# Gathering raw token rows with their mean and reciprocal deviation, instead of stored normalised rows

## The reference, cut to what matters

```python
def _layernorm(x, axis=-1, eps=1e-05):
    m = jnp.mean(x, axis=axis, keepdims=True)
    v = jnp.var(x, axis=axis, keepdims=True)
    return (x - m) / jnp.sqrt(v + eps)

def _L0_ffn_ref(x, router_W, router_b, W1, b1, W2, b2):
    logits = jnp.einsum('bsd,de->bse', x, router_W) + router_b
    probs = jax.nn.softmax(logits, axis=-1)
    mask = jax.nn.one_hot(jnp.argmax(probs, axis=-1), N_EXPERTS)      # 8 experts, top 1
    gates = mask * probs
    h = jax.nn.relu(jnp.einsum('bsd,edf->besf', x, W1) + b1[:, None, :])   # 128 -> 512
    y = jnp.einsum('besf,efd->besd', h, W2) + b2[:, None, :]               # 512 -> 128
    return jnp.einsum('bse,besd->bsd', gates, y)

x = x + 0.5 * _L0_ffn_ref(_layernorm(x, axis=-1), ...)
x = x + _L0_attn_ref(_layernorm(x, axis=-1), ...)
x = x + 0.5 * _L0_ffn_ref(_layernorm(x, axis=-1), ...)
```

## Time and profile before

| what | value |
|---|---|
| time, median of 3 | 206.65 us |
| span of the profiled execution | 213.1 us |
| busy in the span: PE, DVE, ACT, POOL | 188.7, 121.3, 111.6, 122.0 us |
| mean granted TensorE clock | 0.963 |
| DMA: moved, mean rate | 40.26 MB, 189 GB/s |
| chain that ended last, by engine | PE 63%, DVE 13%, issue 9%, POOL 6%, DMA 4%, ACT 2% |

### The profile page before, as it was taken

One profiled execution on the slowest core, in us unless ns is written; L12 is line 12 of the kernel. 1 busy time (PEld: TensorE's weight loads), 2 busy tenths in 40 slices (PEclk: granted clock), 3 DMA queues, 4 the chain that ended last, 5 costly groups with the idle time before them and its releaser, 6 DMA issues.

```text
span 213.1 us, 4561 instructions
## 1 busy us (share of the span) xinstructions
PE 188.7 (89%) x1410; PEld 159.3 (75%) x1410; DVE 121.3 (57%) x516; ACT 111.6 (52%) x328; POOL 122.0 (57%) x186
## 2 busy tenths in 40 slices
PE   4978599997999598898999999998996899999992
PEld 2953269986989597666876588698643899999991
DVE  4858312212212348789897946757531677777762
ACT  2666026644437455778869875131300666666670
POOL 6887456695555526834399704557673154455544
PEclk9976969999999969999999999999999999999998
DMA  5999679764778336169996000001018749676700
GB/s 191 242 381 342 208 249 342 256 197 134 243 174 286 81 85 178 41 259 415 418 410 250 0 2 3 27 28 43 27 63 285 257 165 306 206 264 223 248 27 0
DMA packets 26680, 40.26 MB, mean 189 GB/s; under 512 B 4229, under 2 KB 16296, under 8 KB 25632
## 3 DMA queue, kind: packets, MB, share of 16 engines
q1 hardware_dynamic: 21136, 33.01, 43.9%
q0 software_dynamic: 2496, 4.76, 8.3%
q10 hardware_dynamic: 3024, 2.20, 3.3%
HBM read 10.78 MB, written 14.46 MB: 118 GB/s over the span
## 4 chain that ended last, share of the span: by engine, by line
PE 63%; DVE 13%; issue 9%; POOL 6%; DMA 4%; ACT 2%; another core or an unknown queue 1%; POOLq 0%; DVEq 0%
PE bank L1102 20%; PE bank L1119 18%; PE bank L1238 6%; PE bank L1254 5%; DMA xn_scratch<-xn 3%; PE bank L1095 3%; PE bank L928 2%; DVE stat L1323 2%; POOL xn L581 1%; PE bank L1193 1%; PE bank L1179 1%; DMA Xg<-xn_scratch,srcu 1%; PE bank L1203 1%; DVE x L1558 1%; PE bank L1210 1%
## 5 line engine op out<-in xcount | busy, mean ns | idle before, releaser
L747 ACT ACTIVATE hT<-bank,ewc_own 128x128 f32<-128x128 f32 x184 | 51.6, 373 | 56.7 <-PE bank L1102 38.2
L1102 PE MATMUL bank<-xT,ewc_own 128*128 128x128 f32 x368 | 51.1, 284 | 6.5 <-DVE xT L1455 3.8
L1102 PEld LDWEIGHTS bank<-xT,ewc_own 128*128 128x128 f32 x368 | 46.3, 198 | 9.2 <-issue 9.2
L1119 PE MATMUL bank<-ew,hT 128*128 x368 | 49.4, 278 | 0.0
L1119 PEld LDWEIGHTS bank<-ew,hT 128*128 128x128 f32 x368 | 45.5, 195 | 0.2 <-issue 0.2
L681 POOL DMA_INDIRECT out_dram<-ysb,eqrq x23 | 22.6, 982 | 26.6 <-issue 17.6
L609 POOL DMA_INDIRECT Xg<-xn_scratch,srcu x23 | 22.0, 958 | 15.0 <-PE bank L1102 4.8
L1461 DVE TENSOR_TENSOR ysb<-bank,ewc_own 128x128 f32<-128x128 f32 x23 | 6.7, 289 | 34.1 <-PE bank L1119 26.5
L634 POOL DMA_INDIRECT xnT<-slot_scratch,posu x16 | 15.8, 987 | 13.5 <-DVE ysb L1461 4.3
L928 PE MATMUL bank<-ones_bf 128*128 128x512 bf16 x66 | 19.9, 428 | 3.1 <-POOL ident L499 2.7
L673 POOL DMA_INDIRECT row_scratch<-pay,posu x16 | 15.8, 987 | 10.8 <-DVE posu L1428 6.8
(11 more groups left out here) (239 smaller groups left out, 303.7 us busy)
## 6 DMA issues: line engine op xcount, KB each, us to landing
ewc_own<-ew SPq DMA_DIRECT2D x46, 322.0 KB
row_scratch<-xn SPq DMA_DIRECT2D x8, 1024.0 KB, 10.6
ew<-in_L_ffn_W_dram SPq DMA_DIRECT2D x1, 2048.0 KB, 11.1
slot_scratch<-ysb SPq DMA_DIRECT2D x23, 64.0 KB
ew<-in_L_ffn_W_dram SPq DMA_DIRECT2D x5, 256.0 KB, 9.4
eqrq<-row_scratch SPq DMA_DIRECT2D x18, 70.0 KB
x<-in_L_attn_x_dram SPq DMA_DIRECT2D x4, 256.0 KB, 3.6
xn_scratch<-xn ACTq DMA_DIRECT2D x4, 256.0 KB, 6.2
```

What stands on the lines that cost most here:

```text
L747: last = A(hT[:, t.slot, c * P:(c + 1) * P], up_bank(k, c)[:, c * P:(c + 1) * P], ACT.Relu, scale=0.5 if m else 1.0, bias=ewc[t.ahead][:, ...
L1102: last = mm(up_bank(k, c)[:, c * P:(c + 1) * P], ewc[t.ahead][:, c * P:(c + 1) * P], xT[:, t.slot, :], start=True, stop=True)
L1119: last = mm(bank[4 + t.parity][:, 0:D], hT[:, t.slot, c * P:(c + 1) * P], ew[:, bass.ds(e[k], 1), W2_AT + c * D:W2_AT + (c + 1) * D].squee ...
```

## The change

The first mixture layer now works as the second: a memory tensor `x_scratch` of 130 numbers a row takes the raw row, its mean and its reciprocal deviation, and VectorE normalises each gathered tile.

- SP copies x from the input to `x_scratch` in four transfers from memory to memory (rows of 512 bytes at a pitch of 520), after the first-layer weights and ahead of its five second-layer loads.
- ACT stores mean and reciprocal deviation of each group (`store_stats`, 512 pieces of 8 bytes each) between its copies; GpSimd writes the reciprocal deviation into `mv`, beside the mean.
- The normalised rows `xn`, their stores, ACT's `renormalise`, GpSimd's share of it and VectorE's `first_shift` go. Gathers go to `Xp`, a buffer that the second time uses too, and wait for the copies, the statistics and the list.
- `normal` runs in both expert stages, in the first one or two tiles ahead.
- ACT loads the second-layer weights of the last three experts only after the first tile's own weights have landed.
- In `ranks`, the four products that need later constants (two lines) move behind the first half's rank products, the wait of the first half is for fewer constants, and a product that only kept TensorE busy goes.
- GpSimd makes its masks and other constants before its three row-hit products, not after them. The constant rows that fill memory come from a buffer `filler`.

```diff
+XW = D + 2
-    xn_scr = nc.dram_tensor("xn_scratch", [TOK, D], f32, kind="Internal").ap()
+    x_scr = nc.dram_tensor("x_scratch", [TOK, XW], f32, kind="Internal").ap()
...
             sp.dma_start(ew[:, :, W1_AT:W1_AT + F], ew1_d.rearrange("e p f -> p e f")).then_inc(ew_in, 16)
+            for g in range(NG):
+                sp.dma_start(x_scr_v[:, g, :, 0:D], x_v[:, g, :, :]).then_inc(x_copied, 16)
             load_w2(sp, range(NE - W2_BY_ACT))
...
-            for t in range(POOL_ROWS * GT, (POOL_ROWS + 1) * GT):
-                last = g.tensor_scalar(xn[:, t, :], x[:, t, :], mv[:, t, 0:1], rstd[:, t, 0:1], ALU.subtract, ALU.mult)
-            last.then_inc(xn_by_pool, 1)
...
-                    g.indirect_dma_start(out=Xg[:, k % UNROLL, :], out_offset=None, in_=xn_scr,
+                    g.indirect_dma_start(out=Xp[:, k % UNROLL, 0:XW], out_offset=None, in_=x_scr,
...
-                for b in range(NG):
-                    pool.wait_ge(xn_stored[b], 16)
+                pool.wait_ge(x_copied, 16 * NG)
+                pool.wait_ge(stats_stored, 16 * NG)
                 pool.wait_ge(src_ready, 1)
...
+            def store_stats(g):
+
+                act.wait_ge(rstd_ready, g + 1)
+                act.dma_start(x_scr_v[:, g, :, MEAN_AT:XW], mv[:, g * GT:(g + 1) * GT, :]).then_inc(stats_stored, 16)
...
-            for g in range(NG):
+            take_xn(0, 0)
+            for g in range(1, NG):
                 take_xn(0, g)
-            renormalise(0)
-            renormalise(1)
-            store_xn(0)
-            store_xn(1)
-            renormalise(3)
-            store_xn(3)
-            store_xn(POOL_ROWS)
+                store_stats(g - 1)
+            store_stats(NG - 1)
             exponentials()
             row_hits()
+            act.wait_ge(ewc_in[0], 16)
             load_w2(act, range(NE - W2_BY_ACT, NE))
...
-                pe.wait_ge(const_ready, 10)
-                mm(bank[5][0:NV, 0:1], whole[:, :], ones_v[0:1, 0:1], start=True, stop=False, skip_group_check=True)
-                mm(bank[5][0:NV, 2:4], ident[0:NV, 0:NV], add_step[:, :], start=False, stop=False, skip_group_check=True)
+                pe.wait_ge(const_ready, 5)
...
                 for t in range(PICKED):
                     spread(t)
-                keep_warm(1)
+                pe.wait_ge(const_ready, 10)
+                mm(bank[5][0:NV, 0:1], whole[:, :], ones_v[0:1, 0:1], start=True, stop=False, skip_group_check=True)
+                mm(bank[5][0:NV, 2:4], ident[0:NV, 0:NV], add_step[:, :], start=False, stop=False, skip_group_check=True)
                 pe.wait_ge(oh_ready, picks(0))
...
-                    if m == 0:
-                        pe.wait_ge(g_in[t.ahead], 16 * (1 + t.round))
-                    else:
-                        pe.wait_ge(xg_ready, t.k + 1)
+                    pe.wait_ge(xg_ready, m * NT + t.k + 1)
...
-                    dve.wait_ge(xp_in[t.ahead], 16 * (1 + t.round))
+                    dve.wait_ge((xp_in if m else g_in)[t.ahead], 16 * (1 + t.round))
...
+                normal(0)
                 take_x(0)
-                if m == 1:
-                    normal(1)
+                normal(1)
                 take_x(1)
-                if m == 1:
-                    normal(2)
+                normal(2)
                 for k in range(NT):
...
                     for n in ups_before_down(m, k):
                         if n + 1 < NT:
                             take_x(n + 1)
+                        if m == 0 and n + 2 < NT:
+                            normal(n + 2)
```

53 lines of the change are left out of this document (14 added, 39 removed).

## The result

The changed kernel takes 216.21 us (median; 215.71 to 216.98), the kernel before 206.64 beside it: a ratio of 1.048, 95% interval 1.0446 to 1.0515. It is 9.6 us slower, where 0.45 us faster was forecast, and far above the range of 204.9 to 208.3.

What follows compares the result with a forecast made beforehand. TensorE's successive matmuls were taken as the bound, loads mattering only before the first down products. Matmuls (31.0) and weights (31.2) plus hand-over gave 31.25 against 31.72: 206.65 - 0.45 = 206.2 us, range 204.9 to 208.3.

Steps and rivals of the forecast that it cites:

- The mark: Start of the first down products on TensorE, 31.72 us before; its shift was taken to last to the end.
- The rank products: Routing stage: reordered products bring the hits product from 14.83 to about 13.90 us and the list to 20.93.
- The normalising between turns 1 and 2: TensorE's first tiles: turn 2 waits for VectorE's copy 1 and normalise 2, some 0.9 us.
- From the last second-layer issue to the first tile load: SP's queue: reading the codes and issuing takes 2.45 us as today, so first tile load at about 21.75.
- ScalarE's loads hanging on that landing: Last three experts' second-layer loads held until first tile weights land at 24.9 us; last issue begins at 26.0.
- The weights: Deciding term, before the first down products: held second-layer loads land at 31.2 us, against 31.0 for the matmuls.
- I take 3.2: SP's raw-row copies of 1 MB to memory: 3.2 us, between 2.7 and a landing after 10.6.
- The statistics: Stores of 2048 pieces of 8 bytes: 1.0 us taken, between nothing and 3.2.
- A copy that takes 5 us: Condition in the late-weights rival: copies at 5 in place of 3.2 us give the same 208.4 us.
- the next one's: Rival that the gather does not move, starting at 24.02: copy of 6 us, 208.05 us; chance counted within late weights' 0.32.
- I take a half share: ScalarE's three held loads beside seven tile loads: 4.6 us at 170 GB/s plus 0.6, from 26.0 to 31.2.
- The weights come late: Rival: copies and 8-byte pieces delay first tile weights, held loads follow, TensorE stands at down 0; 208.4 us, chance 0.32.

Runs made afterwards that it cites:

- e5: e2 with rows of `x_scratch` 576 bytes apart in place of 520, statistics filling the last 64 bytes: 213.19 us (1.0312).
- e6: e2 with the raw rows stored from the x already on the core, not copied from memory, still at a pitch of 520 bytes: 217.46 us (1.0494).
- e10: Changed kernel with whole rows stored in 2080-byte pieces, hold kept, loads of tile 3 and later issued only after all second-layer weights landed: 209.68 us (1.0176).
- e11: e10 with five products of ones added on TensorE between the turns of tiles 1 and 2: 208.9 us (1.0138).
- e16: Changed kernel with ten products of ones on TensorE in its wait before the first down products: 215.43 us (1.0413).
- e2: Changed kernel with the four statistics stores issued only after the four copies have landed: 215.46 us (1.0396).
- e13: Changed kernel, hold and order kept, with rows of `x_scratch` 576 bytes apart in place of 520: 213.06 us (1.0276).
- e12: Changed kernel with SP issuing loads of tile 3 and later only after all second-layer weights have landed: 214.85 us (1.0355).
- e14: e13 with SP issuing loads of tile 3 and later only after all second-layer weights have landed: 211.62 us (1.0223).
- e15: Changed kernel with rows 576 bytes apart and without ScalarE's hold of the last three second-layer loads: 210.86 us (1.0184).
- second profile of before: The kernel before, unchanged, run and profiled once more: 207.69 us, span 206.0.
- e7: Changed kernel with whole rows stored from the core in 2080-byte pieces, no copies and no hold: 210.8 us (1.0193).

## Why the prediction was wrong

*What was right.* The mark: the loss is there by the first tiles. The rank products: hits product 13.75 (13.90 forecast), list at 20.88 (20.93), though only in executions like this one: in e5, e6, e10, e11 and e16, with the same order of products, the hits product came at 15.4 to 16.1 behind router products of 2.7 to 3.4 us (1.95 here). The normalising between turns 1 and 2: a wait of 0.64 us (0.9). From the last second-layer issue to the first tile load 2.46 us (2.45), from there to landing 2.94 (3.1). ScalarE's loads hanging on that landing, with TensorE standing at the first down products.

*The step that failed* is the one called decisive, "The weights", by two of its terms.

First, the copies: "I take 3.2 (the stretch in which small pieces run, 324 to 346 GB/s)". SP's last second-layer issue ended 9.0 us later than before (24.09 against 15.1), where 1.0 + 3.2 = 4.2 had been forecast. The statistics are 1.3 of this (that issue ended at 22.77 in e2), near the 1.0 taken. The copies are the other 7.7 in place of 3.2. The 3.2 was worked out from pieces that end on the core; these were written to memory at a pitch of 520 bytes, which no row of before showed. e5, e6 and e13 show that the pitch made them dear: with 576 bytes the issue ended at 19.66 (e5), 3.1 earlier than in e2. So 4.6 us are left at the even pitch; why that is 1.4 above the 3.2 is not shown. "A copy that takes 5 us" was among the rival's conditions, 6 among the next one's; the bounds reached to 10.6, but the range did not follow them. The gather, which waits for the copies too, started at 25.27 in place of 21.9.

Second, the loads: "I take a half share: 0.79 MB at 170 GB/s is 4.6 us, plus 0.6, from 26.0". From the last issue (30.6) they took 9.05 us, which is 87 GB/s, while the engines moved 246 GB/s up to 34.4 us and 359 behind: between a quarter and a third, not a half. The row for it was there, 3.8 to 11.8 us; I took a value near its lower end. e12 and e14 show that the tile loads beside them are part of it.

*The rival that came true* is "The weights come late", by its mechanism. Its rule (each microsecond after 24.9 moves the 31.2) with the landing at 29.5 gives 35.8; the other 3.9 us to 39.65 are the second term. Its price of 208.4 was too small because it moved the landing by 2.2 us, where 4.6 came, and left the time of the held loads as it was.

*Not foreseen at all:* the lower clock behind a long wait (1.4 us, read in the traces of the changed kernel and e16): the sum ended at the start of the down products, and the forecast named the clock only for the first up products. And one of the 23 normalise products did make TensorE wait: that of the last tile stands on VectorE behind the first work of the attention, 1.10 us at 78.87; most of it is made up again, since the next stage waits for the rows brought back, not for that tile (from it to the first turn of the second expert stage 85.8 us, 164.70 - 78.87, against 86.9, 155.75 - 68.85).

*What stays open.* With even pitch and no hold (e15) the span is 2.5 us above the second profile of before, which the rows explain: first turn 1.2, TensorE's own way to the down products 0.9 (the wait for the normalising, the lower clock), 0.7 behind them up to the 22nd tile, less 0.3 later. The medians differ by 4.7, with executions that spread over some 2 us in both kernels; that rest is not settled. Nor is what the 512-byte pieces at a pitch of 520 wait for, nor why the held loads still need 6.41 of their 9.05 us when the tile loads from tile 3 on are kept from beside them (e12).

## What to carry to other kernels

Before a scratch layout is made narrow, look at what each piece writes: here 512-byte pieces in rows 520 bytes apart took the rate of the whole stretch to 163 to 197 GB/s, where rows 576 apart gave 295, and the queue behind them paid for it. In a stretch where the DMA engines are full, an earlier issue is not an earlier landing: count the bytes that must move before the step in question, and ask which transfers nobody needs yet run beside them. When a wait is forecast, price the clock behind it too.

## What the runs showed of the hardware that was not expected

The stretch from 14.3 to 20.8 us, with all that ran in it, moved 163 to 197 GB/s where 512-byte pieces were written to memory in rows 520 bytes apart (e6, e2), and 295 with rows 576 apart (e5); with whole rows in 2080-byte pieces (e7) it moved 369. A source on the core was no faster than one in memory (163 against 197).

The granted clock behind a wait cost as much as some of the waits: from 39.9 to 46.0 us it was 0.75 in the changed kernel, 1.00 in e16. Behind 5.54 us of standing the first group of eight products took 2.07 us and the next 1.32, where 0.89 is the later pace; behind 5.15 us in e13 three groups took 2.07, 1.91 and 1.35. Behind the 1.06 us in the second profile of before the group took 1.16, and behind the wait that e16 filled with products, down to 1.81 us, 1.15.

The kernel before itself spread from 204.8 to 208.9 us over these runs, and the intervals of the comparisons reach 0.3 to 1% to each side, so the 0.2% that the prediction took for a measurable difference was too fine.
